# Routing and scattering tokens in two halves, in a layer of attention and 16 experts

## What is computed

```python
d = x.shape[-1]
xr = x.reshape(-1, d)
S = xr.shape[0]
E = Wg.shape[1]
C = (S + E - 1) // E
gate = jax.nn.softmax(xr @ Wg, axis=-1)
idx = jnp.argmax(gate, axis=1)
gates_s = jnp.take_along_axis(gate, idx[:, None], axis=1)[:, 0]
onehot = jax.nn.one_hot(idx, E, dtype=jnp.int32)
loc = jnp.sum((jnp.cumsum(onehot, axis=0) - 1) * onehot, axis=1)
valid = loc < C
...
h = jax.nn.relu(jnp.einsum('ecm,emf->ecf', dispatched, w1))
expert_out = jnp.einsum('ecf,efm->ecm', h, w2)
gathered = expert_out[idx, jnp.minimum(loc, C - 1)]
combined = gathered * (gates_s * valid.astype(x.dtype))[:, None]
...
x = x + attention(xn) + experts(xn)
```

## Time and profile before

| what | us |
|---|---|
| median of 3 runs | 1205.86 |
| lowest and highest of them | 1204.91, 1207.9 |
| time of the profiled execution | 1205.22 |
| span of the profiled execution | 1203.5 |
| busy over the span: PE, DVE, ACT, POOL | 1072.3, 999.0, 1010.1, 825.2 |

### The profile page before, as it was taken

The page is one execution under the profiler, slowest core; times in us unless marked ns, Lnnn a source line. Parts: engine busy times, 40 slices in busy tenths (PEclk is TensorE's granted clock), DMA queues, the critical chain, the costliest instruction groups (busy, mean ns, idle before and its releaser), DMA issues.

```text
span 1203.5 us, 35533 instructions
## 1 busy us (share of the span) xinstructions
PE 1072.3 (89%) x14451; PEld 774.9 (64%) x14451; DVE 999.0 (83%) x2034; ACT 1010.1 (84%) x2011; POOL 825.2 (69%) x482
## 2 busy tenths in 40 slices
PE   3523999997899999999999899999999999999884
PEld 2413988886466766666666566667666666667653
DVE  8765999994888888888889788888888888898872
ACT  4695998993599989889999889888998989998981
POOL 4173100000789988898899788889988988899731
PEclk8765999998999999999999999999999999999996
DMA  8874667761148556655766676575577657756563
GB/s 265 296 229 142 230 220 251 238 218 45 36 80 156 101 101 139 128 94 118 148 99 108 109 146 98 99 143 123 96 127 142 105 100 138 128 106 112 109 118 70
DMA packets 390322, 165.80 MB, mean 138 GB/s; under 512 B 340754, under 2 KB 380703, under 8 KB 390160
## 3 DMA queue, kind: packets, MB, share of 16 engines
q1 hardware_dynamic: 377136, 143.22, 55.8%
q0 software_dynamic: 4352, 12.41, 3.2%
q10 hardware_dynamic: 8672, 7.90, 2.2%
HBM read 58.79 MB, written 21.00 MB: 66 GB/s over the span
## 4 chain that ended last, share of the span: by engine, by line
PE 45%; DMA 11%; ACT 8%; POOL 5%; issue 3%; SPq 1%; DVE 1%; POOLq 0%; ACTq 0%
PE ps_x L1421 9%; PE ps_o L1498 9%; PE ps_s L1465 9%; DMA pt_dma<-prob_parts 8%; PE ps_t L1478 7%; PE ps_x L1431 5%; PE ps_x L1440 5%; ACT prob L1218 5%; DMA ot<-ctx_parts 3%; POOL prob_parts L1093 2%; ACT pt_pe L1202 2%; POOL ctx_parts L1101 1%; SPq L1037 1%; POOL parts L1087 1%; ACT val_hi L1181 1%
## 5 line engine op out<-in xcount | busy, mean ns | idle before, releaser
L1218 ACT ACTIVATE prob<-prob,neg_max 128x512 f32<-128x512 f32 x512 | 364.0, 714 | 4.7 <-DVE neg_max L1339 2.6
L1339 DVE CUSTOM_DVE_ANT_0 prob<-ps_s,strips,score_scale 128x512 f32<-128x512 f32 x512 | 359.9, 745 | 5.0 <-PE ps_s L1465 3.4
L1093 POOL TENSOR_TENSOR prob_parts<-prob,prob_parts 128x1024 f16<-128x1024 f32 x128 | 273.6, 2138 | 51.8 <-ACT prob_parts L1208 51.5
L1465 PE MATMUL ps_s<-parts 32*128 32x512 f16 x3072 | 190.0, 377 | 1.1 <-DVE parts L1385 1.0
L1345 DVE SCALAR_TENSOR_TENSOR pt_pe<-ps_t,pt_pe 128x1024 f16<-128x1024 f32 x128 | 155.9, 1218 | 36.0 <-ACT pt_pe L1202 36.0
L1478 PEld LDWEIGHTS ps_t<-ident,prob 128*128 128x128 f32 x1024 | 110.5, 142 | 57.1 <-issue 39.0
L1083 POOL TENSOR_TENSOR rot<-prods 128x1024 f32<-128x1024 f32 x61 | 144.4, 2367 | 2.7 <-DVE prods L1305 2.7
L1421 PE MATMUL ps_x<-xcur,wqkv_hi 128*128 128x512 f16 x480 | 143.3, 380 | 2.8 <-DVE pt_dma L1305 1.3
L1478 PE MATMUL ps_t<-ident,prob 128*128 128x128 f32 x1024 | 140.7, 281 | 2.4 <-DVE pt_pe L1345 2.3
L1208 ACT CAST prob_parts<-prob 128x1024 f16<-128x1024 f32 x128 | 133.6, 1044 | 2.0
L1202 ACT ACTIVATE pt_pe<-ps_t 128x1024 f16<-128x1024 f32 x128 | 130.7, 1021 | 4.9 <-PE ps_t L1478 4.8
(11 more groups left out here) (206 smaller groups left out, 2609.2 us busy)
## 6 DMA issues: line engine op xcount, KB each, us to landing
raw<-in_L_ffn_w_dram SPq DMA_DIRECT2D x32, 1024.0 KB, 7.0
xa<-in_L_attn_x_dram SPq DMA_DIRECT2D x8, 512.0 KB, 8.8
xt_dram<-xth SPq DMA_DIRECT2D x8, 512.0 KB, 5.6
slots_dram<-zeros SPq DMA_DIRECT2D x4, 1024.0 KB, 10.3
xa<-slots_dram SPq DMA_DIRECT2D x16, 256.0 KB, 5.3
expert_dram<-xa POOLq DMA_DIRECT2D x16, 256.0 KB, 6.2
xcur<-xt_dram SPq DMA_DIRECT2D x8, 512.0 KB, 4.3
res<-in_L_attn_x_dram ACTq DMA_DIRECT2D x8, 512.0 KB, 4.1
```

The lines of the kernel that those rows point to most:

```text
L1093: nc.gpsimd.tensor_tensor(prob_parts[:, n % 2, 1], prob[:, (2 * n + 1) % 3], prob_parts[:, n % 2, 0], ALU.subtract).then_inc(prob_lo, 1)
L1218: nc.scalar.activation(prob[:, s % 3, q, :], prob[:, s % 3, q, :], ACT.Exp, bias=neg_max[:, 2 * (s % 3) + q:2 * (s % 3) + q + 1], scale=-1 ...
L1339: nc.vector.tensor_tensor_reduce(prob[:, s % 3, q, :], ps_s[u][:], strips[:, HG * j + u, start:start + S], score_scale[:, 0:1], 3.0e38, AL ...
L1465: last = nc.tensor.matmul(ps_s[h][:], parts[rows, 2 * F % 5, a, f, t * P:(t + 1) * P], parts[rows, (2 * F + 1) % 5, c, f, :], start=(i == ...
```

## The change

The routing is cut into halves of 16 tiles. In the list of DVE the first half's `hot(0)`, `keep_counts(0)` and `place(0)` stand inside the loop over `x`, around `normalise` of the last group; PE's `places(0)` stands in iteration 5 of the loop. POOL starts the first 16 scatters when `placed` is 1, and the other 16 when it is 2. The zeros are stored by POOL's queue, two DMAs behind its tiles of group 0 and two behind those of group 1. All logits now pass through `psw[0]`, so `logits_of(b)` waits for ACT's copy of the logits before it (`logits_sb`). Loads of weights stand behind stores 0, 2, 4 and 5; two of ACT's four `squares` follow the loop. `ORDER` runs the weight steps by quarters of `raw`, and each of the four loads of raw weights for experts 0 and 1 waits for its own quarter. On ACT three heads' `logs` come before the weight steps, five behind them, and eight in the experts' loop; all four `squares` of experts 0 and 1 come in a row; the sines move to experts 8 to 10 and DVE's `cosines` to expert 12.

```diff
@@ on_sync
+            if b in WEIGHTS_BEHIND[0:3]:
+                q = WEIGHTS_BEHIND.index(b)
...
-        sp.wait_ge(w_ps, NW + NWO)
         for r in range(2):
             sp.wait_ge(xt_stored[r], 16 * (NB // 2))
         for r in range(2):
             for w in range(2):
+                sp.wait_ge(w_ps, (NW + NWO) // 4 * (2 * r + w + 1))
                 load_expert(sp, raw, w, w1, w2, r, r, ld_we[r][w])
@@ on_gpsimd
+            if g < 2:
+                pool.wait_ge(zero_ready, 1)
+                for i in range(2 * g, 2 * g + 2):
+                    rows = slots_dram[i * 1024:(i + 1) * 1024, :].rearrange("(p r) m -> p r m", p=P)
+                    pool.dma_start(rows, zeros[:].unsqueeze(1).to_broadcast([P, 8, M])).then_inc(slots_zeroed, 16)
         pool.wait_ge(slots_zeroed, 64)
-        pool.wait_ge(placed, 1)
...
+        for h in range(2):
+            pool.wait_ge(placed, h + 1)
...
+            for t in range(h * HALF, (h + 1) * HALF):
+                scatter(nc, slots_dram, scatter_to, xa, t).then_inc(scattered, 16)
@@ on_scalar
-            if b >= 3 and b < NB - 1:
-                squares(b - 3)
+            if b == 3:
+                squares(0)
+            elif b == 5:
+                squares(1)
         keep_logits(NB - 1)
+        squares(2)
+        squares(3)
+        logs(act, range(1, 4))
@@ on_vector
+        statistics(GROUPS - 1)
+        hot(0)
+        transposed_low(NB - 4)
+        keep_counts(0)
+        normalise(GROUPS - 1)
+        place(0)
+        transposed_low(NB - 3)
         angles()
@@ on_tensor, logits_of(b)
-            if b >= 2:
-                pe.wait_ge(logits_sb, b - 1)
+            if b:
+                pe.wait_ge(logits_sb, b)
@@ experts, on_scalar
-                if e < 4:
-                    logs(act, (((13 + e) % H),))
+                if e < H - 8:
+                    logs(act, ((9 + e) % H,))
+                elif e < H - 5:
+                    sines(act, e - H + 8)
...
-        logs(act, range(1, 9))
+        squares(0, 0)
+        squares(0, 1)
```

More of the change, by code:

```diff
@@ L118, in layer @@
                 experts_on = experts(nc, sem, second, w1, w2, slots_dram, expert_dram, ident, ones, raw, xa, scatter_to, scattered,
[L119 removed]
+                                     ld_we, xt_dram, xcur, x_loaded, o_stored, strips, coef, coef_ready, ln_ready, prepare_on["sines"], prepare_on["cosines"], prepare_on["logs"],
                                      prepare_on["routes"])
@@ L238, in prepare @@
     NWO = H * D // P // 2
+    ORDER = [k * (NW // KT) + 2 * third + c for third in range(3) for k in range(KT) for c in range(2)] + list(range(NW, NW + NWO))
     logits = psg[:].rearrange("p a (t e) -> p (a t) e", e=EP)[:, :, 0:E]
@@ L370, in on_scalar @@
         nc.scalar.activation(rt[:, 2], rt[:, 1], ACT.Exp).then_inc(exps, 1)
-        act.wait_ge(ang_ready, 1)
-        nc.scalar.activation(sin, ang[:], ACT.Sin).then_inc(sin_ready, 1)
-        nc.scalar.activation(nsin, ang[:], ACT.Sin, scale=-1.0).then_inc(sin_ready, 1)
-        nc.scalar.activation(cos, ang[:], ACT.Sin, scale=0.5).then_inc(sin_ready, 1)
-    def logs(act, heads):
-        act.wait_ge(dist_cast, 1)
-        act.wait_ge(slope_ready, 1)
-        for h in heads:
-            nc.scalar.activation(strips[:, h, :], strips[:, 0, :], ACT.Ln, bias=1.0,
-                                 scale=slope[:, h:h + 1]).then_inc(ln_ready, 1)
+        logs(act, range(4, 9))
     def on_vector(dve):
@@ L449, in on_vector @@
         normalise(0)
-        for g in range(1, GROUPS):
+        dve.wait_ge(ld_small, 16 * 6)
+        nc.vector.tensor_scalar(slope[:], slope[:], 0.01, None, ALU.max).then_inc(slope_ready, 1)
+        for g in range(1, GROUPS - 1):
             statistics(g)
@@ L538, in turn_logits, with places @@
             nc.tensor.transpose(psg[:, b // 4, at:at + P], turned_logits[:, b % 2], ident[:]).then_inc(logits_ready, 1)
+        def places(h):
+            pe.wait_ge(onehot_ready, h + 1)
+            pe.wait_ge(const_ready, 3)
+            at = 2 * P * h
+            for c in range(2):
+                last = nc.tensor.matmul(psw[1][:, c * P:(c + 1) * P], onehot[:, at + c * P:at + (c + 1) * P], onesh[:], start=True, stop=True)
+            last.then_inc(counted, 1)
+            if h:
+                pe.wait_ge(sq_done, 4)
+                pe.wait_ge(shifted, 1)
+                nc.tensor.matmul(psg[:, 0, E:E + 4], ones[:], wsq[:], start=True, stop=True).then_inc(n2_ready, 1)
+            pe.wait_ge(counts_sb, h + 1)
+            nc.tensor.matmul(psw[1][:, 2 * P:4 * P], before[:], onehot[:, at:at + 2 * P], start=True, stop=False)
+            for c in range(2 * h + 2):
+                later = SW - S - c * P + at
+                last = nc.tensor.matmul(psw[1][:, 2 * P:4 * P], counts[:, c // 2, c % 2 * P:c % 2 * P + P], later_tiles[:, later:later + 2 * P],
+                                        start=False, stop=(c == 2 * h + 1))
+            last.then_inc(located, 1)
         def turn_weight(i):
@@ L565, in on_tensor @@
                 turn_logits(b - 2)
+            if b == NB // 2 + 1:
+                places(0)
         logits_of(NB - 1)
         turn_logits(NB - 2)
-        pe.wait_ge(sq_done, 4)
-        nc.tensor.matmul(psg[:, 0, E:E + 4], ones[:], wsq[:], start=True, stop=True).then_inc(n2_ready, 1)
         turn_logits(NB - 1)
@@ L573, in on_tensor @@
             turn_weight(i)
-        pe.wait_ge(onehot_ready, 1)
-        pe.wait_ge(const_ready, 3)
-        for c in range(4):
-            last = nc.tensor.matmul(psw[0][:, c * P:(c + 1) * P], onehot[:, c * P:(c + 1) * P], onesh[:], start=True, stop=True)
-        last.then_inc(counted, 1)
-        nc.tensor.matmul(psw[1][:], before[:], onehot[:], start=True, stop=False)
-        pe.wait_ge(counts_sb, 1)
-        for c in range(4):
-            last = nc.tensor.matmul(psw[1][:], counts[:, c, :], later_tiles[:, SW - S - c * P:SW - c * P], start=False, stop=(c == 3))
-        last.then_inc(located, 1)
+        places(1)
         for i in range(3, NW + NWO):
@@ L587, in on_tensor @@
         pe.wait_ge(shifted, 1)
-    return {"sync": on_sync, "routes": routes_are_stored, "gpsimd": on_gpsimd, "scalar": on_scalar, "logs": logs,
+    return {"sync": on_sync, "routes": routes_are_stored, "gpsimd": on_gpsimd, "scalar": on_scalar, "sines": sines, "cosines": cosines, "logs": logs,
             "vector": on_vector, "tensor": on_tensor}
@@ L615, in experts @@
 def experts(nc, sem, ctx, w1, w2, slots_dram, expert_dram, ident, ones, raw, xa, scatter_to, scattered, ld_w, xt_dram, xcur,
-            x_loaded, o_stored, strips, coef, coef_ready, ln_ready, logs, routes_are_stored):
+            x_loaded, o_stored, strips, coef, coef_ready, ln_ready, sines, cosines, logs, routes_are_stored):
     FT = F // P
@@ L757, in one @@
             before_rows = isinstance(e, int) and e < 0
-            if before_rows:
-                squares(n + 1, r)
-                if r == 0:
-                    logs(act, range(9, 13))
             if there(e + 1):
@@ L838, in one @@
                 rows_low(*nxt)
+            if e == H - 4:
+                cosines(dve)
         over_experts(one, lead=1)
```

117 lines of the change are left out of this document (71 added, 46 removed).

## The result

The changed kernel took 1192.84 us in the median of 4 runs (1189.7 to 1193.81), the kernel before 1205.86 in 4 runs beside it: ratio 0.989, interval 0.987 to 0.991. The forecast was 1191.4. The profiled execution has a span of 1191.9 us where the one before had 1203.5, 11.6 less.

What follows compares the result with a forecast made beforehand. Routing and scatters ahead of PE's first product bound the kernel, with a weights' chain ending 10 us earlier. 15.1 us gained there less 0.6 in the experts' loop: 1205.86 - 14.5 = 1191.4 us, range 1187.5 to 1199.

Steps and rivals of the forecast that it cites:

- The scatters' chain: Logits, addresses, 32 scatters, rows: first scatter at 44.8, 16.0 us earlier, last ending at 87.0, PE's first product at 93.8.
- 43.5 to 46.5: Window in us for the start of POOL's first scatter, named as a sign that the forecast is right.
- the traffic itself does not grow: Zeros during the loop over x: same traffic, 4 MB down at about 40 us, five ahead of the first scatter.
- The 32 scatters: POOL's scatters: 40.9 us plus 1.3 for long ones, 42.2 in all; 43.4 without escaping DVE's weights.
- rival 1: Scatters from about 45 to 55 us slow down beside full DMA engines: 8.4 us more, 1197.7 us; 13%.
- The zeros on POOL: Each zero store costs POOL 2.85 us (bounds 0.71 and 7.8), covered by its idle time, so cost nothing.
- Rival 2: Zero stores on POOL are dear: at 7.8 us each the loop is 20.2 late, 1211.6 us, 7%; middle price 1198.5, 5%.
- rival 3: Zeros land only near 60 us, so the routing's halves don't help: PE's product at 109, 1204.5 us; 4%.
- The second chain: ACT's squares and DVE's weights before expert 0: weight steps 60.5, squares 81.5, low weights done 95.1, PE's product 95.9.
- The margin between the chains: At PE's first product: scatters would allow 93.8 us, weights 95.9; the later decides.
- The mis-sized term: Experts' loop: added logs, sines and cosines cost 0.6 us, bounds 0 and 1.8, with 0.6 free per expert on DVE.
- The sines: On ACT in the experts' loop: expert 8 gets a load and a sine, 1.9 against 1.5 us free, experts 9 and 10 0.6.

Runs made afterwards that it cites:

- wait_both: Changed kernel with POOL's first 16 scatters also waiting for the second half's addresses (placed at 2): 1209.66 us, ratio to the kernel before 1.0028.
- scatters_alone: Changed kernel with weight-step order, load waits, logs, sines and squares put back as before; scatters, zeros and routing kept: 1202.13 us, ratio to the kernel before 0.9977.
- cosines_again: Changed kernel with DVE's cosines alone moved to expert 15, run on a third chip: 1189.33 us, ratio to the kernel before 0.9857.
- after_again: The changed kernel itself without an edit, run again on a third chip: 1191.36 us, ratio to the kernel before 0.9869.
- sines_last: Changed kernel with the three sines at expert 14 and the cosines at expert 15, on a second chip: 1216.06 us, ratio to the kernel before 1.0095.
- cosines_last: Changed kernel with the cosines alone moved to expert 15, on a second chip: 1213.29 us in a single execution.
- zeros_by_sp: Changed kernel with the four zero stores issued by SP instead of POOL: 1218.47 us on a second chip, 1194.64 us on a fourth.

## Why the prediction came out as it did

**The scatters' chain** was right in kind and 1.3 us off. The first scatter started at 47.02, not 44.8, just outside the 43.5 to 46.5 that I had named. DVE's first half of the routing started at 38.33 instead of 35.8, behind 2.08 us of waiting for PE's transposed logits:

```profile
38.33 0.42 DVE L483 TENSOR_REDUCE col<-psg 128x16 f32<-128x256 f32 x1 [2.08 <-PE psg L590]
...
43.44 2.73 POOL L300 TENSOR_SCALAR xa<-xa,moments,sd 128x256 f32<-128x256 f32 x2 [11.60 <-DVE shift L433]
```

The second of these lines is a wait that the prediction had not named: POOL's own last tiles, behind DVE's shift, end at 46.17, 0.05 us behind the addresses (46.12), so the first scatter could not have started earlier by earlier addresses alone. The lateness comes from ACT, in its line of waits (us in total, times, longest), first of the kernel before, then of the changed one, both from 0 to 60 us:

```profile
ACT xth L350 <- DMA xt_dram<-xth: 2.6, 2, 2.3
```

```profile
ACT xth L382 <- DMA xt_dram<-xth: 8.4, 4, 3.5
```

ACT's float16 copy waits for an older store of the turned `x`, and what stands behind it, the copy of the logits, waits too. The step "the traffic itself does not grow" was true of bytes and false of their place: 4 MB of zeros now move while the loop over `x` runs, from 15.5 us on, together with a quarter of weights. That this wait stays with the zeros on SP (8.0) and with late scatters (7.6 in `wait_both`) clears POOL and the scatters. That the bytes now on the way are the cause is argued and not shown: which share of it the zeros have, and which the weights' new places behind the stores, was not taken apart; a kernel without zeros wasn't tried.

The 32 scatters took 41.26 us, not 42.2. The sum had put 40.9 for scatters of the median length, where 32 x 0.974 + 31 x 0.30 is 40.5, and 1.3 for the long ones, which came to 0.7. The two above 1.10 us, 1.24 and 1.15 at 76.62 and 78.17, lie beside DVE's angles, which have both inputs in SBUF:

```profile
75.61 2.86 DVE L465 SCALAR_TENSOR_TENSOR ang<-turns,ang 128x512 f32<-128x512 f32 x4
```

This is what the Trainium skill says in "GPSIMD Engine Reference", section "Key points" (GpSimd contends with VectorE's instructions that have two SBUF inputs); the trace agrees, with 0.2 to 0.3 us per scatter here, where the one of 2.02 us in the earlier trace rows had DVE's low weights beside it. It is no fixed price: in the kernel before, the scatter at 98.32 took 0.97 beside the same weights. That late scatters are long again in `wait_both` (43.37 us in all), and early ones are not (41.26), bears out that scatters which end ahead of DVE's weights escape that cost. It is 2.1 us, where the prediction had 1.2 (43.4 and 42.2). The scatters that ran between 47 and 55 us, beside a DMA share of 0.91, took 0.97 like the rest, but for the first two (1.10 and 1.04): rival 1 (full DMA engines lengthen them) is out.

**The zeros on POOL**: 0.94 us each, not 2.85. The row I scaled by the number of rows (0.712 for 256 of them) does not scale so: four times the rows cost 1.3 times as much. The measured price lay beneath my value and above the lower bound of 0.71, and since POOL's idle time was to cover nearly all of even 2.85 the term in the sum stayed 0. Rival 2 (dear zeros) is out, rival 3 (zeros that land late) too: the first scatter starts 0.90 us behind the addresses, as before (0.94).

**The second chain** came as summed: weight steps at 60.92 (60.5 forecast), squares at 81.82 (81.5), low weights done at 95.10 (95.1), PE's product at 95.85 (95.9). The logits were a little later than forecast (52.53 on ACT, 52.2 forecast; 53.22 on DVE, 52.7), which is the 0.4 us of the weight steps. The margin between the chains was not as summed: 2.1 us in the forecast (93.8 and 95.9), within half a microsecond in the runs, since the scatters ended 1.3 later. That the second chain still decided was close to luck. What the prediction had not seen is a condition of it: without the early squares of expert 1, PE's list would have held expert 0 back (105.55 in `scatters_alone`).

**The mis-sized term** is the experts' loop, 0.6 forecast and 2.05 measured. This is above the prediction's own upper bound of 1.8. I read the earlier trace rows as 0.6 us free per expert on DVE (112.21 of 119 busy). It is not free. DVE's timeline of `cosines_again`, which has no cosines here, one expert from `n_e` to `n_e`:

```profile
243.39 0.15 DVE L849 COPY n_e<-psn_e 128x2 f32<-128x2 f32 x1
243.57 0.17 DVE L60 TENSOR_SCALAR expo_e<-n_e 128x2 int32<-128x2 int32 x1
243.78 0.17 DVE L61 TENSOR_SCALAR expo_e<-expo_e 128x2 int32<-128x2 int32 x1
243.98 0.17 DVE L62 TENSOR_SCALAR expo_e<-expo_e 128x2 int32<-128x2 int32 x1
...
251.05 3.67 DVE L869 SCALAR_TENSOR_TENSOR wlo<-raw,scale_e,whi 128x1024 f16<-128x1024 f32 x3
254.63 0.15 DVE L849 COPY n_e<-psn_e 128x2 f32<-128x2 f32 x1
```

There is no bracket with idle time in it: DVE goes round in 254.63 - 243.39 = 11.24 us without a wait. Steps of 0.17 us stand 0.20 apart, and with such gaps this round shows 10.90 us busy of 11.24, which is 97%. The 94% of the earlier trace rows is a mean over unlike parts. In the kernel before each round of 11.24 us from 180 to 270 has 10.88 to 10.90 busy, and only 3.65 of the last 7 us, from 280 on, where DVE has no weights left. So what looked like 0.6 us free per expert was for the most part the end of the loop. PE has no idle time in this round either (11.24 of 11.24), so both engines are full, and what is put on DVE is paid nearly in full: in the changed kernel's round with the cosines PE waits 0.78 us for DVE. In the changed kernel the cosines stand in this round:

```profile
244.22 0.68 DVE L330 TENSOR_TENSOR trig<-trig 128x512 f32<-128x512 f32 x1
244.93 0.43 DVE L332 TENSOR_SCALAR trig<-trig 128x512 f32<-128x512 f32 x1
245.28 0.15 DVE L849 COPY n_e<-psn_e 128x2 f32<-128x2 f32 x1
...
256.50 0.15 DVE L849 COPY n_e<-psn_e 128x2 f32<-128x2 f32 x1
```

ACT's copies out tell the cost, since one stands in each expert. Of the changed kernel:

```profile
244.22 0.67 ACT L811 ACTIVATE xa<-pso,un_e 128x512 f32<-128x512 f32 x1
256.48 0.67 ACT L811 ACTIVATE xa<-pso,un_e 128x512 f32<-128x512 f32 x1
```

and of `cosines_again`:

```profile
243.37 0.67 ACT L811 ACTIVATE xa<-pso,un_e 128x512 f32<-128x512 f32 x1
254.61 0.67 ACT L811 ACTIVATE xa<-pso,un_e 128x512 f32<-128x512 f32 x1
```

12.26 against 11.24: 1.02 us for the cosines. The two kernels' other gaps agree within 0.05, but for two: 11.62 against 11.02, where the changed kernel's ACT waited 0.81 us for a raw weight in this one execution (in `after_again` it is 10.89), and 11.05 against 11.24 right ahead of the cosines. All traces say the same: from the first copy out to the last, the seven others with the cosines at expert 12 (not counting `scatters_alone`) took 166.45 to 167.18 us, the changed kernel 166.87, the four with the cosines at expert 15 165.46 to 165.53, and the kernel before 165.13. The sines, for which I had feared more, cost nothing: the four gaps around them are 11.94, 10.53, 11.02 and 10.33 in `cosines_again`, 43.82 in all, and four of the plain 11.24 less the step from log experts to others, which the kernel before makes too (10.01 instead of 11.14), give 43.83. In `sines_last`, with the sines at expert 14, the same four gaps are 43.78 in all. So of the 2.05, 1.02 are the cosines, 0.31 the way from the first product to the first copy out (14.68 and 14.99; over all executions it varies from 13.8 to 15.3), 0.6 the one late weight, and 0.1 remains. The late weight and the way to the first copy out were found and not tested; they differ between executions of the same kernel.

**The total** came out nearer than its parts. The forecast span was 1189.0 and the measured one 1191.9, 2.9 longer: 1.45 from the loop, 0.33 from the step to attention and 1.14 from attention itself, for which the forecast had nothing. The median is only 1.4 above its forecast because the profiled execution lay 0.83 us above its median here and 0.64 below it before; that part is luck.

**What the range did not hold.** 1187.5 to 1199 was made of this kernel's own mechanisms. On one of the four chips of the experiments, four of its near relatives took 1213 to 1221. The changed kernel itself was not run there, and what makes the engines stand still is open: that the file of `cosines_last` took 1213.29 there and 1189.33 elsewhere, and that of `zeros_by_sp` 1218.47 and 1194.64, shows that it is not these two edits; whether it is the chip, or the time at which the four ran, was not taken apart; and that the kernel before took 1206.17 there shows that it needs something of the changed one. Scatters beside the loop and the weight steps are the obvious candidate, but no run shows it.

## What to carry to other kernels

Where two chains meet at one start, cost both before an order is changed, and look at every list between them: here moving the longer chain by 16 us was worth 3.7 until the other, and an unrelated sum in front of PE's rows, were moved too. A busy share of 94% over a long stretch can hide an engine that is full (97% busy, no wait) in all of it but the end: look in the timeline for brackets with idle time before counting on room, and put extra steps where such brackets are. Bytes moved to an earlier place can be a cost there even if their number is the same: here the stores beside them were waited for 8.4 us instead of 2.6.

## What was not expected of the hardware

POOL's time for a plain store went by what DVE did beside it more than by its size. The stores of 256 rows took 0.715 us in the median before and twice as much in the changed kernel:

```profile
L766 POOL DMA_DIRECT2D expert_dram<-xa x16: 714/1432/1597, 111.8 to 278.7; - x16
```

In the traces of both kernels each such store that starts together with DVE's `whi` step (`TENSOR_SCALAR`, 128x2048, 1.29 us, one tensor read) takes 1.43 or 1.44 us, one that starts 0.17 us ahead of it takes 1.60, and the rest, which start 0.47 us or more ahead of it or meet none, take 0.71 or 0.72. Four of the 16 stores started so before, nine of them in the changed kernel. The stores of 1024 rows met no such step, only DVE's statistics, and took 0.94 us in the median. POOL idles some 10 us per expert there, and nothing shows that the longer stores cost time.

On one chip of four, PE, ACT and DVE stood still for 3 to 9 us at a time, so that expert 0's squares came some 25 us later, in each of four kernels that scatter early, while the kernel before kept its usual time. Two of the four files ran elsewhere without it; the other two were run only there.
